# One order of steps for each engine, a recurrence with one difference, and normalisations on ScalarE

## The reference

```python
def step(carry, kv_t):                 # over 4096 tokens, per channel; two sequences, 512 channels
    a, b, pp = carry
    kt, vt = kv_t
    ww = u + kt
    q = jnp.maximum(pp, ww)
    y = (exp(pp - q) * a + exp(ww - q) * vt) / (exp(pp - q) * b + exp(ww - q))
    ww2 = pp + w
    q2 = jnp.maximum(ww2, kt)
    return ((exp(ww2 - q2) * a + exp(kt - q2) * vt, exp(ww2 - q2) * b + exp(kt - q2), q2), y)
...
x = x + (sigmoid(r) * y) @ Wo          # k, r = layernorm(x) @ Wk, Wr ; v = r
h = rmsnorm(layernorm(x)) * gamma1     # then q, and k and v of a latent
x = layernorm(x) + softmax(q k / sqrt(32)) v @ Wo      # 16 x 16 heads within one token
gate = softmax(h2 @ Wg + bg)           # h2 = rmsnorm(x) * gamma2
out = x + residual + sum_e gate_e * (h2 @ We_e)
```

## Time and profile before

| | |
|---|---|
| median of 3 runs | 3332.1 us (3330.17 to 3335.84) |
| the profiled execution | 3332.17 us |
| its span | 3330.3 us |
| TensorE busy | 2887.2 us, 87% |
| VectorE busy | 2476.6 us, 74% |
| ScalarE busy | 956.6 us, 29% |
| GpSimd busy | 686.1 us, 21% |

### The profile page before, as it was taken

One profiled execution on the slowest core, in us unless ns is written; L12 is line 12 of the kernel. 1 busy time (PEld: TensorE's weight loads), 2 busy tenths in 40 slices (PEclk: granted clock), 3 DMA queues, 4 the chain that ended last, 5 costly groups with the idle time before them and its releaser, 6 DMA issues.

```text
span 3330.3 us, 53600 instructions
## 1 busy us (share of the span) xinstructions
PE 2887.2 (87%) x18864; PEld 1791.2 (54%) x18864; DVE 2476.6 (74%) x4548; ACT 956.6 (29%) x1823; POOL 686.1 (21%) x745
## 2 busy tenths in 40 slices
PE   2359999998888989989998898999889998999889
PEld 2235555554555655555564555555555555555544
DVE  5797777778777768777777777768777777877753
ACT  2243232322332322322331332232233232232320
POOL 0111222212122212222221222221222221212210
PEclk9669999999999999999999999999999999999999
DMA  6011111101111101111111111111111110111110
GB/s 192 15 24 20 33 33 26 30 24 33 20 33 27 33 20 33 20 33 26 33 27 26 20 33 30 29 26 27 27 26 33 27 33 20 32 21 33 26 20 13
DMA packets 588333, 102.96 MB, mean 31 GB/s; under 512 B 556562, under 2 KB 556690, under 8 KB 588050
## 3 DMA queue, kind: packets, MB, share of 16 engines
q1 hardware_dynamic: 588068, 99.40, 16.4%
HBM read 48.49 MB, written 16.78 MB: 20 GB/s over the span
## 4 chain that ended last, share of the span: by engine, by line
PE 62%; DVE 23%; issue 7%; SPq 5%; DMA 2%; ACT 0%; POOL 0%; DVEq 0%; ACTq 0%; POOLq 0%
PE bank L1049 49%; PE bank L1201 6%; DVE mcol L954 4%; SPq L424 4%; DVE zz L865 3%; PE bank L1079 3%; DVE ks L943 3%; DVE wkv L839 2%; PE bank L1191 2%; DMA qs<-m 2%; DVE acc L1028 1%; DVE wkv L827 1%; PE bank L1165 1%; DVE ht L935 1%; DVE zz L832 1%
## 5 line engine op out<-in xcount | busy, mean ns | idle before, releaser
L1049 PE MATMUL bank<-w_e,h2t 128*128 128x512 f16 x6144 | 1479.4, 398 | 19.1 <-DVE acc L1028 19.1
L1049 PEld LDWEIGHTS bank<-w_e,h2t 128*128 128x128 f16 x6144 | 617.9, 103 | 757.5 <-issue 123.1
L1028 DVE SCALAR_TENSOR_TENSOR acc<-bank,gates,acc 128x512 f32<-128x512 f32 x512 | 373.6, 737 | 164.7 <-PE bank L1049 163.6
L1201 PEld LDWEIGHTS bank<-vp,pr 128*128 128x128 f32 x2048 | 263.9, 197 | 24.0 <-DVE hrow L970 3.9
L1201 PE MATMUL bank<-vp,pr 128*128 128x33 f32 x2048 | 259.7, 275 | 3.8 <-ACT pr L608 2.7
L608 ACT ACTIVATE pr<-bank,col 128x512 f32<-128x512 f32 x256 | 171.9, 685 | 316.1 <-PE bank L1191 315.7
L865 DVE RECIPROCAL zz<-zz 128x256 f32<-128x256 f32 x128 | 219.1, 1733 | 46.8 <-POOL zz L462 46.8
L1049 PE MATMUL bank<-w_o,xo 128*128 128x512 f16 x768 | 174.3, 384 | 58.8 <-DVE xo L799 58.8
L455 POOL TENSOR_TENSOR e<-wkv 128x512 f32<-128x512 f32 x64 | 72.1, 1127 | 645.6 <-DVE wkv L827 645.6
L1191 PE MATMUL bank<-qs,ks 106*128 106x128 f16 x1024 | 104.5, 236 | 113.9 <-DMA qs<-m 113.9
L1182 PE MATMUL bank<-ks,qs 104*128 104x128 f16 x1024 | 90.8, 231 | 125.7 <-DMA ks<-k 65.7
(11 more groups left out here) (177 smaller groups left out, 3918.1 us busy)
## 6 DMA issues: line engine op xcount, KB each, us to landing
qs<-qo SPq DMA_DIRECT2D x384, 64.0 KB, 3.0
xk<-in_attn_x SPq DMA_DIRECT2D x32, 512.0 KB, 3.9
x<-in_attn_x SPq DMA_DIRECT2D x32, 512.0 KB, 3.6
result<-acc SPq DMA_DIRECT2D x32, 512.0 KB, 2.8
ks<-k SPq DMA_DIRECT2D x128, 64.0 KB, 3.0
w_e<-in_ffn_We SPq DMA_DIRECT2D x7, 1024.0 KB, 13.8
qs<-m SPq DMA_DIRECT2D x256, 2.0 KB, 1.7
qs<-in_attn_Wk SPq DMA_DIRECT2D x1, 1024.0 KB, 5.5
```

The costliest lines, as they stand in the source:

```text
L1028: V.scalar_tensor_tensor(out=acc[:, s, :], in0=moe_bank[u % 2][:, :], scalar=gates[:, s, e:e + 1], in1=acc[:, s, :], op0=ALU.mult, op1=ALU ...
L1049: ins = nc.tensor.matmul(dst, left(a), right(b), start=(n == 0), stop=(n == last))
L1201: ins = nc.tensor.matmul(att_bank[ATT_BANK["PV", k]][:, n * (HD + 1):(n + 1) * (HD + 1)], pr[:, k % 2, n * P:(n + 1) * P], vp[:, 4 * k + n ...
```

## The change

1. `ORDER` becomes five lists, one for each engine, which hold the same steps in different places.
2. The recurrence on VectorE takes one difference dd = k - pp (pp is the maximum before the token). The exponents of the decay and of the new value are relu(dd + exp(decay)) and relu(-dd - exp(decay)), made by four ScalarE instructions of 256 columns for each half, and negated in the exponential. `mix_decay` on GpSimd goes away. The limit of the exponent of the current token becomes 64.
3. The output numerator is a + exp(z) v, added on GpSimd (`mix_num`), times the reciprocal; the four VectorE operations around v are replaced by two products in a new step `mix_value`.
4. The layer norms (`pre_norm`, `att_norm`, `att_rest`), the RMS norm (`att_norm2`) and the eviction of v (`att_up`) move from VectorE to ScalarE; VectorE only makes their small bias columns `nb1` and `nb2`.

```diff
+PE_ORDER = [
...
+    ("att_max", 2), ("att_max", 3), ("moe", 6), ("moe", 7), ("moe", 8), ("att_scores", 0), ("att_scores", 1),
+    ("moe", 9), ("att_probs", 0), ("att_scores", 2), ("att_probs", 1), ("att_scores", 3), ("att_probs", 2),
...
+ACT_ORDER = [
...
+    ("att_latent", 0), ("att_q", 0), ("att_up", 0), ("mix_v", 0), ("moe", 2), ("moe", 3), ("mix_exp", 0), ("moe", 4),
+    ("moe", 5), ("moe", 6), ("moe", 7), ("mix_num", 0), ("att_rest", 0), ("att_scores", 0), ("moe", 8), ("moe", 9),
+    ("att_scores", 1), ("mix_split", 0), ("att_scores", 2), ("att_scores", 3), ("att_scores", 4), ("att_scores", 5),
...
+POOL_ORDER = [
+    ("att_stats", 0), ("moe_acc", 0), ("att_q", 0), ("att_up", 0), ("mix_sum", 0), ("mix_num", 0), ("mix_sum", 1),
+    ("att_rest", 0), ("mix_num", 1), ("att_square", 0), ("moe", 15), ("pre_stats", 0),
+]
...
         @block.gpsimd
-            def mix_decay(t, h):
-                pool.wait_ge(*mix_dve.done(t, f"pp_{h}"))
-                nc.gpsimd.tensor_tensor(e1[:, :, :], wkv[:, 0, :, 0:T], wkv[:, 0, :, 1:T + 1], ALU.subtract).then_inc(mix_pool.sem, 1)
-                nc.gpsimd.tensor_tensor(e2[:, :, :], k32[:, HF * h:HF * h + HF, :], wkv[:, 0, :, 1:T + 1], ALU.subtract)\
-                    .then_inc(mix_pool.sem, 1)
...
+            def mix_num(t, h):
+                pool.wait_ge(*mix_dve.done(t, f"a_{h}"))
+                nc.gpsimd.tensor_tensor(ev[:, :, :], wkv[:, 1, :, 0:T], ev[:, :, :], ALU.add).then_inc(mix_pool.sem, 1)
...
         @block.scalar
             def mix_exp(t, h):
-                act.wait_ge(*mix_dve.done(t, f"zc_{h}"))
+                act.wait_ge(*mix_dve.done(t, f"dd_{h}"))
+                for c in range(HF):
+                    nc.scalar.activation(e1[:, c, :], e2[:, c, :], ACT.Relu, bias=ecol[:, HF * h + c:HF * h + c + 1]).then_inc(mix_act.sem, 1)
+                act.wait_ge(*mix_dve.done(t, f"z_{h}"))
+                act.wait_ge(*mix_act.done(t, f"ra_{h}"))
+                for c in range(HF):
+                    nc.scalar.activation(e2[:, c, :], e2[:, c, :], ACT.Relu, bias=wcol[:, HF * h + c:HF * h + c + 1], scale=-1.0)\
+                        .then_inc(mix_act.sem, 1)
+                nc.scalar.activation(e1[:, :, :], e1[:, :, :], ACT.Exp, scale=-1.0).then_inc(mix_act.sem, 1)
+                act.wait_ge(*mix_act.done(t, f"rb_{h}"))
+                nc.scalar.activation(e2[:, :, :], e2[:, :, :], ACT.Exp, scale=-1.0).then_inc(mix_act.sem, 1)
                 nc.scalar.activation(zz[:, :, :], zz[:, :, :], ACT.Exp).then_inc(mix_act.sem, 1)
...
+            def att_norm(t, _):
+                act.wait_ge(*att_dve.done(t, "shift"))
+                if t.back(1):
+                    act.wait_ge(*att_pe.done(t.back(1), "T21"))
+                for s in range(SUB):
+                    nc.scalar.activation(h_rows[:, s, :], x1[t.par][:, s, :], ACT.Identity, bias=nb2[:, 1, s:s + 1], scale=rs2[:, 1, s:s + 1])\
+                        .then_inc(att_act.sem, 1)
...
         @block.vector
+                V.tensor_tensor(e2[:, :, :], k32[:, HF * h:HF * h + HF, :], wkv[:, 0, :, 0:T], ALU.subtract).then_inc(mix_dve.sem, 1)
+                dve.wait_ge(*mix_dve.done(t, f"dd_{h}"))
                 for c in range(HF):
 
-                    V.scalar_tensor_tensor(out=zz[:, c, :], in0=k32[:, HF * h + c, :], scalar=ucol[:, HF * h + c:HF * h + c + 1],
-                                           in1=wkv[:, 0, c, 0:T], op0=ALU.add, op1=ALU.subtract).then_inc(mix_dve.sem, 1)
-                dve.wait_ge(*mix_dve.done(t, f"z_{h}"))
-                V.tensor_scalar(zz[:, :, :], zz[:, :, :], ZMAX, None, ALU.min).then_inc(mix_dve.sem, 1)
+                    V.tensor_scalar(zz[:, c, :], e2[:, c, :], ucol[:, HF * h + c:HF * h + c + 1], ZMAX, ALU.add, ALU.min).then_inc(mix_dve.sem, 1)
...
+            def mix_value(t, h):
+                vh = v32[:, HF * h:HF * h + HF, :]
+                dve.wait_ge(*mix_act.done(t, "v", h))
+                dve.wait_ge(*mix_act.done(t, f"r_{h}"))
+                V.tensor_tensor(ev[:, :, :], zz[:, :, :], vh, ALU.mult).then_inc(mix_dve.sem, 1)
+                dve.wait_ge(*mix_dve.done(t, f"b_{h}"))
+                V.tensor_tensor(e2[:, :, :], e2[:, :, :], vh, ALU.mult).then_inc(mix_dve.sem, 1)
...
             def att_norm(t, _):
-                xa = x1[t.par]
                 dve.wait_ge(*att_pool.done(t, "rstd"))
-                for s in range(SUB):
-                    V.tensor_scalar(h_rows[:, s, :], xa[:, s, :], mv2[:, s, 0:1], rs2[:, 1, s:s + 1],
-                                    ALU.subtract, ALU.mult).then_inc(att_dve.sem, 1)
...
+                for n in range(2):
+                    V.scalar_tensor_tensor(out=nb2[:, n, :], in0=mv2[:, :, 0], scalar=-1.0, in1=rs2[:, n, :], op0=ALU.mult, op1=ALU.mult)\
+                        .then_inc(att_dve.sem, 1)
```

187 lines of the change are left out of this document (92 added, 95 removed).

## The result

| | before | changed kernel |
|---|---|---|
| median | 3332.1 us | 3226.9 us (3209.34 to 3239.68, 4 runs) |
| the profiled execution | 3332.17 us | 3235.43 us |
| its span | 3330.3 us | 3233.6 us |
| mean granted clock | 0.941 | 0.932 to 0.942 |

The change makes the kernel faster, by the ratio 0.968 (95% interval 0.963 to 0.973). The forecast of 3132 us with its range from 3080 to 3205 was too low: of the 200 us expected, 105 came. The direction was right and the size wrong.

The account below looks back on a forecast made before the run. TensorE, busy 87% of the span, was taken as the bound. Its waits and slow clock summed to 89.5 instead of 95.75 us an iteration without the loop's turn, in all 200 us off 3332.2: 3132 us, range 3080 to 3205.

Parts of the forecast that it names:

- The wait of expert step 4: TensorE's 0.52 us wait for an expert step of VectorE goes, 0.7 us from start to start.
- those for the maxima: TensorE's 2.4 us of waiting for the column maxima go in each iteration.
- The wait for k's stack: TensorE's wait of 1.93 us for the stack of k grows by 0.5 us.
- step 7: Expert step 7 on TensorE waits for step 5's addition, which stands behind the maxima on VectorE: 0.9 us come back.
- the scores wait: TensorE's wait for the sent maximum ahead of the scores falls from 4.4 us, start to start, to about 0.1.
- The pairs: Six pairs of values and scores, back to back in the attention's core: 0.6 us of waiting, bounds 0 and 2 us.
- rival 2: Everything fits: no pair is stretched and the iteration's end holds, near 3080 us; chance 0.14.
- The tail: Iteration's end: VectorE's queue 14.5 us against TensorE's 15.0 us; TensorE waits 0.5 us, bounds 0 and 5 us.
- rival 1: VectorE's queue at the iteration's end becomes the bound through GpSimd collisions: near 3196, at most near 3270 us; chance 0.18.
- the term for the clock: The slow clock after TensorE's wait for the sent maximum goes with that wait: 1.36 us less an iteration.
- the loop's turn: Every second iteration, where the loop turns, TensorE has issue idle and some slow clock: 5.75 us a pair, kept.
- rival 3: ScalarE's waits bring the clock down in the six pairs, which lack expert matmuls: +170 us, near 3500 us; chance 0.04.

Follow-up runs that it names:

- e1_moe10_mid: Changed kernel with expert step 10 between the third and fourth pair on TensorE and mix_decay 1 one value product earlier on VectorE: 3206.5 us.
- e12_decay_only: Changed kernel with mix_decay 1 one value product earlier on VectorE and nothing else: 3321.0 us.
- e15_fill_half: Changed kernel with 10 unread matmuls ahead of the wait for k's stack and one of 256 columns ahead of each of the last six score products: 3136.8 us.
- e5_fill_both: Changed kernel with 10 unread 512-column matmuls ahead of the wait for k's stack and one ahead of each of the last six score products: 3161.7 us.
- e2_fill_stack: Changed kernel with 10 unread matmuls of 512 columns ahead of TensorE's wait for k's stack: 3225.8 us.
- e3_fill_core: Changed kernel with one unread matmul of 512 columns ahead of each of the last six score products: 3214.9 us.

## Why the forecast was wrong, point by point

**The waits were right.** The wait of expert step 4 and those for the maxima are gone. The wait for k's stack is 2.20 us in the flat iteration and 2.4 to 3.0 in the loop (2.4 forecast), step 7 waits 0.67 us plus the 0.15 of its last matmul (0.9 forecast), the scores wait 0.59 us in the flat iteration and not at all in the loop's iterations (0.1 forecast). The pairs have no idle time (0.6 forecast): of rival 2, this half holds. By the forecast's terms the 28 iterations would have 181 us idle: 4.8 us in each and 3.4 us at each turn. They have 163.

**The tail was right, though one of its terms was too small.** TensorE waits 0.76 us for `xo`, 0.5 forecast, so rival 1 is out. The collisions that it feared do occur. In the changed kernel's timelines of VectorE and then of GpSimd, two scans take 1.39 us, and the next two 3.28 us beside GpSimd's sums:

```profile
1738.80 1.39 DVE L895 TENSOR_TENSOR_SCAN wkv<-e,wkv 128x256 f32<-128x256 f32 x2
...
1742.60 3.28 DVE L895 TENSOR_TENSOR_SCAN wkv<-e,wkv 128x256 f32<-128x256 f32 x2
```

```profile
1740.85 1.65 POOL L480 TENSOR_TENSOR zz<-wkv,zz 128x512 f32<-128x512 f32 x1 [27.90 <-DVE ev L906]
1742.46 2.88 POOL L493 TENSOR_TENSOR x<-x,bo_row 128x512 f32<-128x512 f32 x2
```

It is the two bias sums (L493) that the slow scans meet. They cost 1.9 us, more than the 1 us allowed, and far from the 5 us of GpSimd's whole work. The Trainium skill ("SBUF — State Buffer", on the shared port pair) lets such instructions exclude each other. These rows agree with it: of the scans of L895, the 196 that meet no sum of GpSimd take 0.75 us at most, the 60 that meet one 1.66 us at least.

**The step that failed is the term for the clock.** The sum took off the 1.36 us behind the wait for the maximum and kept only what it put at the loop's turn, 14 x 2.4 = 33 us. The forecast had 2586.5 us for the 28 iterations (14 x 184.75) and the trace has 2674.5, 88 us more. Slow clock stretches TensorE's work by 125 us and not by 33, which is 92; the idle time is 18 us below the forecast's terms, and 14 us are left, mostly since the flat iteration holds 0.5 us more work and as much less idle time than the sum had. At the turn the trace has 25 us. The rest lies at two places that the sum had at nothing.

In the pairs it is 69 us: rival 3's mechanism, at a fifth of its price (2.5 us an iteration, where it took 11.5 us). It had been priced by waits of ScalarE which never came. And it had been given 0.04 with the argument that "before the pairs stand three expert steps without a gap"; the window at 1722.10 shows the clock falling with TensorE busy all along. The experiments without fillers say the same from the other side: `e1_moe10_mid` moved the slow stretch, and `e12_decay_only` lengthened it.

Behind the wait for k's stack it is 29 us, which were there before. The forecast walked along the iteration at 1623.68, in which the clock stayed up there, and took its 4.22 us of waiting for the maximum as the wait of all; the mean of the 28 is 3.33. In 17 of them the wait was shorter because slow clock stood ahead of it, and that slow clock stays when the wait goes. This is why the idle time fell by 97 us and not by the 137 us that the sum's terms take off, while the stretched work rose and did not fall.

The Trainium skill ("TensorE: Matmul & The Clock Gate", Part 1) says that a block in the hardware watches how busy TensorE has been of late and sets its clock, and names idleness as what takes it down. The falls behind the wait for k's stack agree. For those in the pairs the records have no idle time ahead (10.80 of 10.80 us busy), and the measurement decides: what the profile calls busy can't be all that the clock goes by.

Kept in the forecast's own terms: `e15_fill_half`, in which some 25 us of stretched work are left, has 2588.7 us for the 28 iterations, where the forecast had 2586.5. It holds 2.8 us of fillers an iteration, of which 2.2 stand in the place of the wait for k's stack.

**The ends.** Of the profiled execution's 103 us over the forecast, 88 are in the 28 iterations and 15 outside. Before the first of them the gain was 9 us (340.27 to 331.55) with some 14 forecast; after the last it was 1 us (from 3101.72 to the end 230.5 us, from 3006.04 on 229.4) with 11 forecast. In the last attention iteration expert work waits 5.14 us for VectorE. I did no experiment there. The median of the runs lies 8.5 us below the profiled one.

**How far it is shown.** That lost clock at these two places is worth the missing gain is shown by `e5_fill_both` and `e15_fill_half`: more work and less time. The places and sizes are shown by the ledgers by place, of `e2_fill_stack` and `e3_fill_core` above all. Not shown is what in the narrow products brings the clock down, whether their width, their weight loads or their float32 operands, nor why 4 of the 28 iterations are spared.

## What to carry to other kernels

When a change closes TensorE's waits, its slow clock is no longer paid for by them: compare busy time for the same matmuls between the two traces, piece by piece; read a wait as the mean of many iterations and not in one; and price each remaining wait and each stretch of narrow matmuls with the slow work behind it. Where such a stretch can't be broken up with work that is needed, a few wide matmuls of no use may pay. Move a step of one engine only together with the step of the other that covers it, and try each move alone as well: two edits that gained 20 us together cost 94 and 64 us apart.

## What the runs showed of the hardware that was not expected

- The granted clock fell to the level of 1.2 GHz in a stretch where TensorE was busy for 10.80 of 10.80 us, in narrow products; one matmul of 256 columns a pair (0.11 us) kept it at 2.4 GHz in all 28 iterations of `e15_fill_half`.
- The runs of one kernel differ through it: the four of the changed kernel had clocks of 0.942, 0.939, 0.933 and 0.932 and took 3209, 3218, 3235 and 3240 us, in this order; `e15_fill_half` has 0.969 to 0.970 and 3133 to 3140 us.
- A pair of scans takes 3.28 us where it meets two sums of GpSimd (L493, 2.88 us), and 1.39 us alone. GpSimd's sum of L480, which meets products of VectorE, takes 1.65 us; the same sum had a mean of 1.26 us before.
- One issue of SyncE among the eight of the maximum took 0.75 to 1.91 us and not 0.50 to 0.60 in just the 105 of 476 iterations in which a transfer of instructions (DMA queue 8) began among them.
